# Three places of one kernel reordered: the first projection, the third layer norm with its routing, and the last additions

## The reference

```
x = x + cross_attention(layernorm(x), ctx, ctx, fside)      # 8192 context rows, fside 512x8192 added to the scores
x = x + causal_self_attention(layernorm(x))                 # one head of 512
x = x + mixture(layernorm(x))                               # below

logits = h @ gate_w.T;  scores = softmax(logits);  keep the 2 best of 8 experts per token
out    = sum over the 2 of  score * (silu(h @ G_e.T) * (h @ U_e.T)) @ D_e        # inner width 704
out   += sigmoid(h @ s) * (silu(h @ G.T) * (h @ U.T)) @ D                        # shared, inner width 1408
```

## Time and profile before

| | |
|---|---|
| median of 3 runs | 716.10 us (715.59 to 716.19) |
| the profiled execution | 714.77 us |
| its span in the trace | 713.0 us |
| TensorE matmul busy | 695.7 us, 98% |
| VectorE busy | 554.2 us, 78% |
| ScalarE busy | 336.6 us, 47% |
| GpSimd busy | 193.7 us, 27% |

### The profile page before, as it was taken

The page is one execution under the profiler, slowest core; times in us unless marked ns, Lnnn a source line. Parts: engine busy times, 40 slices in busy tenths (PEclk is TensorE's granted clock), DMA queues, the critical chain, the costliest instruction groups (busy, mean ns, idle before and its releaser), DMA issues.

```text
span 713.0 us, 9901 instructions
## 1 busy us (share of the span) xinstructions
PE 695.7 (98%) x3221; PEld 573.3 (80%) x3221; DVE 554.2 (78%) x701; ACT 336.6 (47%) x450; POOL 193.7 (27%) x144
## 2 busy tenths in 40 slices
PE   6999999999999999999999999899999999999996
PEld 6888888888887788888888888678888788888885
DVE  6488888878989998899995653668334799899896
ACT  4322222222245555566563333633233587887872
POOL 4335444454430000000000000246874111212154
PEclk9999999999999999999999999999999999999998
DMA  8046666776742337422310604322300899999984
GB/s 309 3 159 200 229 214 242 246 225 224 234 132 90 96 111 297 144 89 88 110 37 13 267 1 159 136 89 90 132 2 2 306 340 351 393 389 366 399 284 131
DMA packets 38542, 130.68 MB, mean 183 GB/s; under 512 B 6643, under 2 KB 10485, under 8 KB 35445
## 3 DMA queue, kind: packets, MB, share of 16 engines
q1 hardware_dynamic: 35684, 124.32, 48.9%
q0 software_dynamic: 1536, 4.20, 1.8%
q10 hardware_dynamic: 1296, 1.85, 0.8%
HBM read 120.89 MB, written 9.46 MB: 183 GB/s over the span
## 4 chain that ended last, share of the span: by engine, by line
PE 89%; DVE 7%; issue 2%; ACT 1%; DMA 0%; DVEq 0%
PE ps L892 21%; PE ps L859 8%; PE ps L855 8%; PE ps L856 8%; PE ps L1076 5%; PE ps L811 5%; PE ps L813 5%; PE ps L812 5%; PE ps L1046 4%; PE ps L1057 3%; PE ps L1055 3%; PE ps L1056 3%; PE ps L1063 1%; DVE stats L1171 1%; PE ps L1085 1%
## 5 line engine op out<-in xcount | busy, mean ns | idle before, releaser
L429 POOL TENSOR_TENSOR c_lo<-ring,c_hi 128x512 fp32r<-128x512 f32 x64 | 83.7, 1309 | 105.1 <-ACT c_hi L539 105.1
L539 ACT ACTIVATE c_hi<-ring 128x512 fp32r<-128x512 f32 x64 | 40.4, 633 | 128.1 <-PE ps L859 104.4
L855 PE MATMUL ps<-qk_hi,c_hi 128*128 128x512 f32 x256 | 100.4, 392 | 0.1
L856 PE MATMUL ps<-qk_lo,c_hi 128*128 128x512 f32 x256 | 99.8, 390 | 0.0
L1237 DVE TENSOR_TENSOR runmax<-runmax,att 128x512 f32<-128x512 f32 x64 | 94.2, 1472 | 6.0 <-DVE att L1231 3.2
L434 POOL TENSOR_TENSOR w_lo<-raw,w_hi 128x1024 fp32r<-128x1024 f32 x11 | 26.7, 2423 | 264.4 <-ACT w_hi L666 264.3
L1541 DVE TENSOR_TENSOR wu_lo<-raw_u,wu_hi 128x2048 fp32r<-128x2048 f32 (+1 forms) x33 | 69.7, 2112 | 15.3 <-ACT wu_hi L676 14.8
L859 PE MATMUL ps<-qk_hi,c_lo 128*128 128x512 f32 x256 | 68.5, 390 | 0.0
L892 PE MATMUL ps<-p_hi,d_hi 128*128 128x512 f32 x256 | 64.2, 393 | 0.6 <-DVE ps L1314 0.6
L1231 DVE SCALAR_TENSOR_TENSOR att<-ring,beta,ps 128x512 f32 (+1 forms) x64 | 47.8, 747 | 20.6 <-PE ps L859 20.1
L892 PE MATMUL ps<-p_hi,d_lo 128*128 128x512 f32 x256 | 63.3, 390 | 0.0
(11 more groups left out here) (297 smaller groups left out, 1473.8 us busy)
## 6 DMA issues: line engine op xcount, KB each, us to landing
ring<-stream SPq DMA_DIRECT2D x64, 512.0 KB, 3.6
raw_u<-up_in SPq DMA_DIRECT2D x22, 1024.0 KB, 7.3
raw_d<-down_in SPq DMA_DIRECT2D x33, 512.0 KB, 7.3
ring<-ctx_in SPq DMA_DIRECT2D x32, 512.0 KB, 3.3
raw<-shared_in SPq DMA_DIRECT2D x11, 768.0 KB, 5.1
raw_u<-up_last_in SPq DMA_DIRECT2D x11, 768.0 KB, 6.9
slots<-blank SPq DMA_DIRECT2D x15, 256.0 KB
late<-wqkv_in SPq DMA_DIRECT2D x1, 3072.0 KB, 10.1
```

The lines of the kernel that those rows point to most:

```text
L429: pool.tensor_tensor(c_lo[:, s % 2, :], ring1[:, s, 0, :], c_hi[:, s % 2, :].bitcast(F32), ALU.subtract).then_inc(lo1_ready, 1)
L539: act.activation(c_hi[:, s % 2, :], ring1[:, s, 0, :], ACT.Copy).then_inc(hi1_ready, 1)
L855: pe.matmul(ps[:, s, :], hi, qk_hi[:, k, :], start=(k == 0), stop=False)
L856: pe.matmul(ps[:, s, :], hi, qk_lo[:, k, :], start=False, stop=False)
```

## The change

Line numbers in the listings headed "Now" are those of the changed file; all others are those of the kernel before.

**Opening.** The fillers go from 6, 3, 3, 3, 4 to 6, 3, 4. The high·high part of the query projection is cut into two halves of 256 columns. After two transposed tiles TensorE starts on the first half for k = 0 and 1, transposes the other two tiles, goes on with k = 2 and 3, then takes the second half; the high·low matmuls and the low·high ones follow in blocks. ScalarE splits one piece of the query weights before each transposed tile it reads. GpSimd waits for all four normalized tiles before its first low part. Several small semaphores become one (`key_loaded`).

**Third layer norm.** `WARM3` goes from 5, 4, 4, 1, 5 to 5, 8, 3, and the transposed tiles go to banks 4 to 7. After the second transposed tile TensorE starts the gate and up products of shared experts 0 and 1 on 256 columns (`side_begun`), with the other two transposes between them, and finishes them after the logits (`side_ended`). ScalarE loads the table of the root earlier and runs `shared_high(1)` before the attention's last transposed tile; it reads the first two transposed tiles together and the last two together. On VectorE `moments` moves behind `scales` and `turned_low`.

**Routing.** `token_weights`, `extra_units`, `slot_rows` and `further_units` are spread over the shared experts 0 to 3. GpSimd's scatters come one expert later (rows after the low parts 4, 5, 6; pairs, now 3, 3 and 2, after 7, 8, 9), and its `low_parts(2)` waits for `h_ready`.

**End.** `WARM_END` goes from 7 to 4. The gathered rows of the second choice for tiles 0 and 1 are added before `output_low(1)`, on a semaphore for their own two gathers; GpSimd waits for one scaled tile at a time; the last tile is added and stored in two halves.

```diff
-WARM = (6, 3, 3, 3, 4)
-WARM_END = 7
-WARM3 = (5, 4, 4, 1, 5)
+WARM = (6, 3, 4)
+WARM_END = 4
+WARM3 = (5, 8, 3)
...
+            pool.wait_ge(ln_ready, ST)
...
             for n in range(1, SH):
+                if n == 2:
+                    pool.wait_ge(h_ready, 1)
                 low_parts(n, n % RAW, n % HL)
-                if n == 3:
...
                     scatter_rows(0, 3)
-                if n == 4:
+                if n == 5:
                     scatter_rows(3, 6)
...
+                if n == 6:
                     scatter_rows(6, 8)
-                if 6 <= n < 10:
-                    scatter_info(2 * (n - 6), 2 * (n - 5))
+                if n == 7:
+                    scatter_info(0, 3)
+                if n == 8:
+                    scatter_info(3, 6)
+                if n == 9:
+                    scatter_info(6, 8)
...
+            gather_kept(0, 0, ST, met_full)
+            gather_kept(1, 0, 2, met_second)
+            gather_kept(1, 2, ST, met_rest)
             pool.wait_ge(added, 2 * ST)
-            for st in range(ST // 2, ST):
-                pool.tensor_tensor(x[:, st, :], x[:, st, :], met[:, 1, st, :], ALU.add).then_inc(met_step, 1)
+            for st in range(2, ST):
+                pool.wait_ge(met_step, st - 1)
+                pool.tensor_tensor(x[:, st, :], x[:, st, :], met[:, 1, st, :], ALU.add).then_inc(met_added, 1)
...
             root(1, 0, 0)
             root(1, 1, 1)
+            wq_high(0)
             evacuate_lnT(1, 0, 0, lna_hi, 4)
             root(1, 2, 2)
-            wq_high(0)
+            wq_high(1)
             evacuate_lnT(1, 1, 1, lna_hi, 4)
             root(1, 3, 3)
+            wq_high(2)
             evacuate_lnT(1, 2, 2, lna_hi, 4)
-            wq_high(1)
+            wq_high(3)
             evacuate_lnT(1, 3, 3, lna_hi, 4)
-            wq_high(2)
-            wq_high(3)
...
                     evacuate_pT(n - 1, DOWN[n - 1])
             act.wait_ge(sc_psum, ST)
             shared_high(0)
+            act.activation(std[:, 0:1], ident[:, 0:1], ACT.Sqrt)
             evacuate_pT(ST - 2, DOWN[ST - 2])
+            shared_high(1)
             evacuate_pT(ST - 1, DOWN[ST - 1])
             root(3, 0, DOWN[0])
-            for n in range(ST):
-                if n + 1 < ST:
-                    root(3, n + 1, DOWN[n + 1])
+            for n in range(2):
+                root(3, n + 1, DOWN[n + 1])
                 normal(3, n, DOWN[n])
-                if n >= 1:
-                    evacuate_lnT(3, n - 1, DOWN[n - 1], l_hi, 0)
-            evacuate_lnT(3, ST - 1, DOWN[ST - 1], l_hi, 0)
-            shared_high(1)
+            for n in range(2):
+                evacuate_lnT(3, n, DOWN[n], l_hi, 4)
+            root(3, 3, DOWN[3])
+            for n in range(2, ST):
+                normal(3, n, DOWN[n])
+            for n in range(2, ST):
+                evacuate_lnT(3, n, DOWN[n], l_hi, 4)
             act.wait_ge(logitT_psum, 1)
...
                 act.activation(met[:, 1, st, :], met[:, 1, st, :], ACT.Copy, scale=weight_of[:, 1, st:st + 1]).then_inc(met_step, 1)
-            for st in range(1, ST, 2):
-                act.wait_ge(added, 2 * ST + st + 1 + min(st + 1, ST // 2))
-                act.dma_start(out[st * P:(st + 1) * P, :], x[:, st, :]).then_inc(out_stored, 16)
+            act.wait_ge(added, 2 * ST + 2 + 2)
+            act.dma_start(out[P:2 * P, :], x[:, 1, :]).then_inc(out_stored, 16)
+            act.wait_ge(added, 2 * ST + 2 + 4)
+            act.dma_start(out[3 * P:S, 0:D // 2], x[:, 3, 0:D // 2]).then_inc(out_stored, 16)
         @block.tensor
...
-            for st in range(ST):
+            first_half, second_half = slice(0, S // 2), slice(S // 2, S)
+            def query_high(k, cols, opening=False):
+                for e in range(KC):
+                    pe.matmul(ps[:, e, cols], wq_hi[:, k, e * P:(e + 1) * P], lna_hi[:, k, cols], start=opening, stop=False,
+                              skip_group_check=True)
+            for st in range(2):
                 turn_ln(1, st, st, ln_a, 4)
                 keep_warm(WARM[1 + st], 3)
+            pe.wait_ge(lnT_ready, 2)
+            for k in range(2):
+                pe.wait_ge(wqhi_ready, k + 1)
+                query_high(k, first_half, opening=(k == 0))
+            for st in range(2, ST):
+                turn_ln(1, st, st, ln_a, 4)
+            for k in range(2, KC):
+                pe.wait_ge(wqhi_ready, k + 1)
+                query_high(k, first_half)
             pe.wait_ge(lnT_ready, ST)
+            for k in range(KC):
+                query_high(k, second_half)
             pe.wait_ge(lnT_lo_ready, ST)
             for k in range(KC):
-                pe.wait_ge(wqlo_ready, k + 1)
                 for e in range(KC):
-                    cut = slice(e * P, (e + 1) * P)
-                    pe.matmul(ps[:, e, :], wq_hi[:, k, cut], lna_hi[:, k, :], start=(k == 0), stop=False)
-                    pe.matmul(ps[:, e, :], wq_hi[:, k, cut], lna_lo[:, k, :], start=False, stop=False)
-                    mm = pe.matmul(ps[:, e, :], wq_lo[:, k, cut], lna_hi[:, k, :], start=False, stop=(k == KC - 1))
...
-            for n, st in enumerate(DOWN):
-                keep_warm(WARM3[n], st)
-                turn_ln(3, n, st, rows_n, 0)
-            keep_warm(WARM3[ST], 4)
+            first_half, second_half = slice(S // 2, S), slice(0, S // 2)
+            def side_high(n, part, bank, cols, opening):
+                for k in range(KC):
+                    for w in (w_hi, w_lo):
+                        pe.matmul(ps[:, bank, cols], w[n][:, part, k * P:(k + 1) * P], l_hi[:, k, cols],
+                                  start=(opening and k == 0 and w is w_hi), stop=False, skip_group_check=True)
+            def side_begun(n, part, bank):
+                pe.wait_ge(whi_ready, n + 1)
+                pe.wait_ge(wlo_ready, n + 1)
+                pe.wait_ge(lnT_ready, 2 * ST + 2)
+                side_high(n, part, bank, first_half, True)
+            def side_ended(n, part, bank, done):
+                side_high(n, part, bank, second_half, False)
+                for k in range(KC):
+                    mm = pe.matmul(ps[:, bank, :], w_hi[n][:, part, k * P:(k + 1) * P], l_lo[:, k, :],
+                                   start=False, stop=(k == KC - 1), skip_group_check=True)
+                mm.then_inc(done, 1)
+            keep_warm(WARM3[0], 0)
+            turn_ln(3, 0, DOWN[0], rows_n, 4)
+            keep_warm(WARM3[1], 0)
+            turn_ln(3, 1, DOWN[1], rows_n, 4)
+            keep_warm(WARM3[2], 0)
+            side_begun(0, 0, 0)
+            turn_ln(3, 2, DOWN[2], rows_n, 4)
+            side_begun(0, 1, 2)
+            turn_ln(3, 3, DOWN[3], rows_n, 4)
+            side_begun(1, 0, 1)
+            side_begun(1, 1, 3)
...
-            up_shared(0, between=turn_logits)
-            up_shared(1, between=count_places)
+            side_ended(0, 0, 0, g_psum)
+            turn_logits()
+            side_ended(0, 1, 2, u_psum)
+            side_ended(1, 0, 1, g_psum)
+            count_places()
+            side_ended(1, 1, 3, u_psum)
             pe.wait_ge(counts_read, 1)
...
                 dve.wait_ge(y_psum, n + 1)
                 step(dve.scalar_tensor_tensor(out=x[:, i, :], in0=ps[:, 4 + i, :], scalar=rinv[:, i:i + 1],
                                               in1=x[:, i, :], op0=ALU.mult, op1=ALU.add))
...
             for n in range(2):
                 turned_low(n, DOWN[n])
             dve.wait_ge(probs_ready, ST)
             step(dve.reciprocal(rinv[:, :], rowsum[:, :]))
             for n in range(ST):
-                if n < 2:
-                    turned_low(n + 2, DOWN[n + 2])
                 self_attended(n, DOWN[n])
                 if n >= 1:
                     scales(3, n - 1, DOWN[n - 1])
+                if n < 2:
+                    turned_low(n + 2, DOWN[n + 2])
+                moments(DOWN[n])
             scales(3, ST - 1, DOWN[ST - 1])
...
             step(dve.tensor_reduce(rank[:, :, :], gt, AX_X, ALU.add))
-            dve.wait_ge(gexp_ready, 2)
-            step(dve.tensor_scalar(ex[:, :, E], ex[:, :, E], 1.0, None, ALU.add))
-            dve.reciprocal(gate_col[:, :], ex[:, :, E]).then_inc(gate_ready, 1)
             dve.tensor_scalar(taken16[:, :, :], rank[:, :, :], 2.0, None, ALU.is_lt).then_inc(taken_ready, 1)
-            step(dve.tensor_reduce(rowsum[:, :], ex[:, :, 0:E], AX_X, ALU.add))
-            step(dve.reciprocal(rinv[:, :], rowsum[:, :]))
-            step(dve.tensor_tensor(wn[:, :, 0:E], ex[:, :, 0:E], rinv[:, :].unsqueeze(2).to_broadcast([P, ST, E]),
...
                 step(dve.tensor_reduce(row32[:, :, :], chosen[:, :, :, :], AX_X, ALU.add))
                 step(dve.tensor_copy(row_of[:, :, :], row32[:, :, :]))
...
+                    add_met(1, 0, 2)
...
+                if n == 2:
                     slot_rows()
+                if n == 3:
+                    further_units()
```

(11 more changed lines are left out.)

85 lines of the change are left out of this document (49 added, 36 removed).

## The result

The changed kernel takes 709.1 us (median of 4 executions, 708.4 to 710.1) where the kernel before, measured beside it, takes 715.9 (715.5 to 716.2): a ratio of 0.9908, 95% interval 0.9896 to 0.9920. Measured once more later, on another chip, it gave 708.2 us and 0.9892 (0.9876 to 0.9909). The forecast was 708.7, a ratio of 0.9897.

A forecast was written before the change was run, and what follows sets the result against it. TensorE, busy 695.7 of 713.0 us, was taken as the bound, with gains only where it lacked useful work. 1.7 + 2.9 + 0.5 + 2.3 = 7.4 us off the 716.10 median gave 708.7, range 707.3 to 711.7.

The forecast's parts named there:

- A: Whole kernel: all four pieces gain as worked out, 708.7 us, reaching from 707.4 to 709.8; chance 0.58.
- Opening, 1.7: Opening: query products start earlier in halves, so the query is through at 23.0 us; 1.7 us less, bounds 1.2 and 2.1.
- read at about 10.4: Opening: ScalarE, alternating weight splits and tile reads, has the second transposed tile read at about 10.4 us.
- Third layer norm, 2.9: Third layer norm: logits 0.75 us later, 3.46 saved behind them, 0.2 for fillers; 2.9 us less, bounds 2.4 and 3.5.
- Case B: Third layer norm: GpSimd's low part starts first and holds up VectorE's `nmr`; gain there 1.0, total 710.6 us; chance 0.30.
- Scatters, 0.5: Shared expert 4: low parts ahead of the scatters remove TensorE's hole; 0.5 us less, bounds 0 and 0.5.
- what is late next: Shared experts: scatters and two low parts take 7.4 of an expert's 8.2 us, so nothing piles up.
- End, 2.3: End: fewer fillers, earlier additions of gathered rows and an earlier GpSimd start; 2.3 us less, bounds 1.5 and 2.6.
- Case D: Stretches lacking fillers: TensorE's clock falls, each 512-column product costs 0.227 us more; 20 us of it gives 718.7; chance 0.03.

The follow-up runs named there:

- e1: The kernel before with the opening of the change alone: 714.2 us, ratio 0.9976.
- e10: The kernel of e9 with ten instead of six fillers ahead of the first transposes: 707.3 us, ratio 0.9885.
- e5: The changed kernel with GpSimd's three iotas moved behind its low part of shared expert 1: 710.4 us, ratio 0.9926.
- e7: The changed kernel without GpSimd's wait on `h_ready` before its low part of expert 2: 709.5 us, ratio 0.9930.
- e8: The changed kernel with the scatters back in the rows of the kernel before, ahead of expert 4's low part: 712.2 us, ratio 0.9948.
- e12: The changed kernel with no fillers in the third layer norm: 710.4 us, ratio 0.9925.
- e13: The changed kernel itself measured once more, against the kernel before: 708.2 us, ratio 0.9892.
- e2: The kernel before with the change's third layer norm, routing in parts and later scatters, without its opening and end: 712.1 us, ratio 0.9953.
- e9: The changed kernel with ScalarE's high part of wq's last quarter ahead of its evacuation of the third turned tile: 708.4 us, ratio 0.9902.
- e3: The kernel before with the scatters one expert later and nothing else: 715.9 us, ratio 1.0004.
- e11: The kernel of e9 with two fillers fewer in the third layer norm and one fewer at the end: 708.3 us, ratio 0.9903.

## Why the prediction was right, and where not

**Sum and case.** 7.4 us were forecast, 6.6 and 7.7 measured in two comparisons, 6.4 between the two profiled executions. The case was A.

**Opening, 1.7.** The term holds for the time: 1.7 (1.0 to 2.4) in e1. Between the two profiles it is 1.0, and the step at fault is the second transposed tile "read at about 10.4". From there to the first key product the prediction had 12.6 us, the trace has 12.63. But the products began 0.7 later, at 11.12: the tile was read by 10.87 and the fillers lasted until 11.12, because transposes and fillers ran at half rate until about 10.6. I had taken their pace from the earlier trace rows's execution, in which TensorE was at full rate from 7 us on. That was the exception: of the fourteen profiles only that one and e10's show it. With the old opening the first key product came at 24.75, 25.15, 25.21 and 26.18, with that of the change at 23.43 to 24.69 (the change, e1, e5, e7, e8, e12, e13; mean 24.08). The means differ by 1.2; among the profiles whose products speed up between 10 and 11 us it is 1.6 (25.15 and 25.21 against 23.43, 23.61 and 23.75).

**Third layer norm, 2.9.** Measured 2.96 and 2.97, and both parts of the sum fit: the logits 0.4 us later behind the closing fillers where the sum had 0.55, and 3.37 less behind them where it had 3.46. What I missed is a condition: without GpSimd's wait on `h_ready` 1.2 of it is lost (e7).

**Case B at 0.30.** Its mechanism is shown by e5. Its price is not: e5 starts GpSimd 0.8 us ahead, so `nmr` lost 1.4 and the stage 1.3, where the prediction had 1.9 for a GpSimd that is first by a hair; that e5's 710.4 us lie so near the 710.6 of the prediction is chance. That the case did not happen in the change was near: the two starts fall in the same hundredth of a microsecond. For the prediction it was luck, since its sum put both starts within 0.1 us and could not tell their order. For the chip it is not: in nine profiles with this stage of the change (all but e5) `nmr` starts 0.00 to 0.02 us ahead and takes 0.16, and in the six that leave the stage unaltered (the change, e2, e8, e9, e10, e13) it takes 20.86 or 20.87. Why the order repeats is not shown.

**Scatters, 0.5.** 0.59 was gained and the hole at expert 4 is gone, as predicted; 0.45 of it lay there (starts 0.60 and 0.30 apart where 0.23 is usual). But "what is late next" was wrong for the edit by itself. It is VectorE's cast and subtraction beside GpSimd's low part (e3), and by the traces it is the routing in parts that takes them apart. I had costed the edits one by one where they are one; that the total came right is partly luck.

**End, 2.3.** It is 2.0 (7.83 or 7.84 in the ten profiles that have the new end, 9.81 or 9.82 in the four that have the old one; in e11 the end is as long with one filler fewer). Two steps were small: the last products start 1.03 behind the fillers' start and not 0.87, because their input, which the prediction held to be there by then, is ready only at 0.88 (699.70) and the product follows 0.15 later; and the end comes 2.75 behind the last addition where I kept 2.6. The last products to VectorE's end took the 4.0 of the prediction (4.05).

**Case D at 0.03.** Not seen in the change. Its price was far off: e12, with 3.2 us of idle time in three holes where the prediction feared 2, lost 1.4 us. Its 0.244 us per filler record has the latency of the last one in it; the starts of the earlier trace rows's first twelve lie 0.21 apart.

## What to carry to other kernels

Before a start is costed from one profile, ask at which clock that execution ran it: here the same instructions moved by up to 1.4 us between executions, nearly what the edit of the opening was worth. Fillers pay ahead of the first useful work (e10's four more: 1.5 us of the opening) and inside it (all of the third layer norm's: 1.4 us). Where GpSimd subtracts in SBUF beside VectorE, plan the order of starts and not the durations, and cost edits that move either engine together: one of these was worth 0 alone and 3.6 us beside its neighbour. The fastest kernel of this study is e10, 707.3 us, 8.2 us (1.15%) under the kernel before; its four executions lie between 706.9 and 707.8, the change's eight between 707.4 and 710.1, so the two overlap.
